# Moving the rank products behind the inverse transform, and reordering GpSimd's record and norm work around the wait for them

## The chip, the cores and the metric

The kernel runs on one core of one Trainium2 chip. The metric is the time of one execution on the device in microseconds (us), the median of several runs. Engines are named as in the profile: PE (TensorE matmuls), PEld (its weight loads), DVE (VectorE), ACT (ScalarE), POOL (GpSimd), SP (SyncE, which only issues transfers here).

## The reference, cut to what matters

```python
# x (64, 256, 257, 2), K (512, 512), W (7, 160, 160)
coeff = complex(x[..., 0], x[..., 1]) * sqrt_eig
h = irfft(einsum('nlm,mlk->nkm', coeff, pct), n=512, norm='forward')   # (64, 256, 512)

xn = layernorm(h)                      # first norm
key = xn @ K
logits = tanh(key @ xn^T + bias)       # 256 x 256 for each of the 64 blocks
logits = (logits - 10000 * outside_band) * temperature
h = h + softmax(logits) @ xn

x2 = layernorm(h)                      # second norm
mask = (x2[..., 0] >= 0.5) & (x2[..., 1] >= 0.5)
# of the tokens in the mask: four argmax over 16 columns of (x2 > 0.5), and column 29,
# through a 7-layer network of width 160; its two rounded results, as one-hot vectors
# times 2, are added to columns 128 to 159
h = h + x2 + add_where_mask(mask, ...)
```

Only tokens in the mask need the network. So the kernel gathers a record of 40 numbers for each of them into a dense list in HBM, and runs the network over that list.

## The kernel before, in words

There are three stages, one after the other. `stage1_spectrum` computes the Legendre sums and writes the spectrum `spec` to HBM; it streams about 200 MB. `stage2_blocks` takes the 64 blocks (256 tokens by 512 numbers each, kept as two tiles of 128 rows) through the inverse transform, the first norm, the attention, the second norm and the output, and writes the records. `stage3_ffn` runs the network over the records and scatters its results. The change touches `stage2_blocks` alone.

Stage 2 is a software pipeline. Each engine has its own program, a function `slot(i, k, has)`, called for i = -2 to 66 (slots 7 to 58 in a hardware loop of four slots a turn; k = i mod 4 picks buffers). `has(n)` is true where block n exists. The order of the work within a slot is the order in which `slot` writes it, and every engine executes its own list strictly in that order; semaphores tie the engines together. In slot i the engines work on different blocks at once:

- PE (L504): the keys of block i (48 products), the rank products of block i-3 (`rank`, L475), the transposed probabilities of i-1 (`probs_T`), the inverse transform of i+2 (`inverse_dft`, 16 products), the transposed input of i+1 (`x_T`), attention times values of i-1 (`attend`), the logits of i (24 x 2 products).
- ACT (L529): tanh of the logits of i-1 (L534) into `th`; exponentials `pr` of i-1 (L541); `keyhi` of i (L547); the copy of the ranks of i-3 out of PSUM into `pos` (L553); `pThi` of i-1 (L557); `xnhi` of i+1 (L562); `od` of i+2 (L568); `xThi` of i+1 (L574); the output `o` of block i-2 (L587), which needs the second norm's scale `sc2` and shift `sh2` from POOL.
- DVE (L595): temperature and row maximum of `lg` (L601), then `h2` = attention plus `h` of i-2 (L612), `xn` of i+1 (L623), `keylo` (L630), `pTlo` (L637), statistics of `h2` (L644), the sums and differences `eo` of the transform (L652), mean and variance `mv2` of block i-2 (L660), `h` of i+2 (L667, L669, L672), `xTlo` (L680), its statistics (L689), `x2` (L697), `mv1` (L706), `wb` (L712), `xnlo` (L719), `v4` (L723).
- POOL (L738): `lg` = `th` + `band` of i-1 (L743); variance plus epsilon and its power -1/2 for the first norm (L748, L751); `nmx`, the negated maxima (L755); for block i-3 the mask and its running counts (L761 to L769: `above`, `mask3`, `acc3`); then the records of block i-3 (L775 to L806, see below); then for block i-2 the second norm's root and what ACT's output needs: `ve` (L811), `rstd2` (L814), `sc2` (L818), `off` (L819), `sh2` (L821).
- SP (L403): loads the next spectrum block and stores `o`.

The ranks: `rank` multiplies the mask of block i-3 by a triangle of ones and the running count by a matrix of ones, both of 3 columns, into the first three columns of the logits' PSUM tile `ps_l`. It waits for the mask counts of POOL (`pool_mask`) and for ACT having read the previous logits (`act_tanh`). ACT copies the result to `pos`. POOL turns it into the row number of each token's record:

```python
pool.wait_ge(dve_v4, n + 1)     # L780
pool.wait_ge(act_pos, n + 1)    # L781: the wait for the ranks
nom  = FAR - FAR * mask3        # L783 (tokens outside the mask go far out of bounds)
fidx = pos + nom                # L786
idx  = uint32(fidx)             # L789
rec[:, r4, :, 0] = rows         # L790, then L791, L793, L796: the record's other fields
rows += NLAT * 16               # L801
for t in range(TILES):          # two indirect transfers, L803
    indirect_dma(recs[idx[:, t]] <- rec[:, t])
```

Of the kernel before, what the change touches and what calls it, by code (L numbers as in the profile page):

```python
# [12 lines left out]
ALU = mybir.AluOpType  # L13
# [4 lines left out]
TILES = NLAT // P  # L18
# [22 lines left out]
def wait(eng, sem, value):  # L41

    if isinstance(value, int) and value <= 0:
        return
    eng.wait_ge(sem, value)
# [204 lines left out]
def stage2_blocks(nc, const, spec, recs, out):  # L250


    with ExitStack() as ctx:
# [126 lines left out]
        def settled(eng):  # L380

            eng.nop(nofuse=True)
# [40 lines left out]
        def _(pe):  # L423
# [51 lines left out]
            def rank(n, k):  # L475

                pe.wait_ge(pool_mask, n * 4 + 4)
                pe.wait_ge(act_tanh, n + 3 if not isinstance(n, int) else min(n + 3, NB))
                nc.tensor.matmul(ps_l[:, 0, 0:3], trib[:, :], mask3[:, k % 2, :], start=True, stop=False)
                nc.tensor.matmul(ps_l[:, 0, 0:3], ones[:, :], acc3[:, k % 2, :],  # L480
                                 start=False, stop=True).then_inc(pe_rank, 1)
# [22 lines left out]
            def slot(i, k, has):  # L504
                if has(i):
                    keys(i, k)
                if has(i - 3):
                    rank(i - 3, (k + 1) % 4)
                if has(i - 1):
                    probs_T(i - 1)  # L510
                if has(i + 2):
                    inverse_dft(i + 2, (k + 2) % 4)
                if has(i + 1):
                    x_T(i + 1, (k + 1) % 4)
                if has(i - 1):
                    attend(i - 1, (k + 3) % 4)
                if has(i):
                    logits(i, k)
# [8 lines left out]
        @block.scalar  # L527
        def _(act):
            def slot(i, k, has):  # L529
                if has(i - 1):  # L530

                    act.wait_ge(pe_logit, i)
                    wait(act, pool_l, i - 1)
                    nc.scalar.activation(th[:, :, :], ps_l[:, :, :], ACT.Tanh,  # L534
                                         bias=bias[:, 0:1]).then_inc(act_tanh, 1)

                    act.wait_ge(pool_nmx, i)
                    wait(act, pe_pT, i - 1)
                    wait(act, dve_rsum, i - 3)
                    for t in range(TILES):  # L540
                        nc.scalar.activation(pr[:, t, :], lg[:, t, :], ACT.Exp, bias=nmx[:, t:t + 1],  # L541
                                             accum_out=ssum[:, (k + 1) % 2, t:t + 1]).then_inc(act_exp, 1)
                if has(i):
                    for b in range(2):
                        act.wait_ge(pe_key, i * 2 + b + 1)
                        wait(act, pe_logit, i)
                        nc.scalar.copy(keyhi[:, 2 * b:2 * b + 2, :].rearrange("p e w -> p (e w)"),  # L547
                                       ps_kx[b][:, :]).then_inc(act_keyhi, 1)
                if has(i - 3):
                    n = i - 3  # L550
                    act.wait_ge(pe_rank, n + 1)
                    wait(act, pool_idx, (n - 1) * 3)
                    nc.scalar.copy(pos[:, (k + 1) % 2, :], ps_l[:, 0, 0:3]).then_inc(act_pos, 1)  # L553
                if has(i - 1):
                    act.wait_ge(pe_pT, i)
                    wait(act, pe_av, (i - 1) * 2)
                    nc.scalar.copy(pThi[:, :, :], ps_pT[:, :, :]).then_inc(act_pThi, 1)  # L557
                if has(i + 1):
                    n = i + 1
                    act.wait_ge(dve_xn, n * 2 + 2)  # L560
                    wait(act, pe_av, (n - 3) * 2)
                    nc.scalar.copy(xnhi[:, (k + 1) % 4], xn[:, (k + 1) % 2]).then_inc(act_xnhi, 1)  # L562
                if has(i + 2):
                    n = i + 2
                    for t in range(TILES):
                        act.wait_ge(pe_dft, n * 2 + t + 1)
                        wait(act, dve_eo, (n - 1) * 4 + 2 * t + 2)
                        nc.scalar.copy(od[:, t, :], ps_dft[t][:, HALF:NLON]).then_inc(act_od, 1)  # L568
                if has(i + 1):
                    n = i + 1  # L570
                    for t in range(TILES):
                        act.wait_ge(pe_xT, n * 2 + t + 1)
                        wait(act, pe_logit, n - 1)
                        nc.scalar.copy(xThi[:, (k + 1) % 2, :, t * P:(t + 1) * P],  # L574
                                       ps_kx[t][:, :].rearrange("p (d w) -> p d w", d=CH)).then_inc(act_xThi, 1)
                if has(i - 2):

                    n = i - 2
                    act.wait_ge(pool_sc2, n * 3 + 3)
                    act.wait_ge(dve_h2, n * 2 + 2)  # L580
                    wait(act, pool_rec, (n - 1) * 4)
                    if isinstance(n, int):
                        wait(act, out_stored[k % 2], 16 * (n // 2))
                    else:
                        act.wait_ge(out_stored[k % 2], n * 8 - 8 * (k % 2))
                    for t in range(TILES):
                        nc.scalar.activation(o[:, k % 2, t], h2[:, k % 2, t], ACT.Identity,  # L587
                                             bias=sh2[:, k % 2, t:t + 1],
                                             scale=sc2[:, k % 2, t:t + 1]).then_inc(act_out, 1)

            slots(nc.scalar, slot)
# [145 lines left out]
        def _(pool):  # L737
            def slot(i, k, has):  # L738
# [34 lines left out]
                if has(i - 3):  # L773

                    n, r4, r2 = i - 3, (k + 1) % 4, (k + 1) % 2  # L775
                    if isinstance(n, int):
                        wait(pool, rec_sent[r4], 32 * (n // 4))
                    else:
                        pool.wait_ge(rec_sent[r4], n * 8 - 8 * r4)
                    pool.wait_ge(dve_v4, n + 1)  # L780
                    pool.wait_ge(act_pos, n + 1)  # L781
                    settled(pool)
                    nc.gpsimd.tensor_scalar(nom[:, :], mask3[:, r2, 0:2], -FAR, FAR, ALU.mult,  # L783
                                            ALU.add).then_inc(pool_idx, 1)
                    pool.wait_ge(pool_idx, n * 3 + 1)
                    nc.gpsimd.tensor_tensor(fidx[:, :], pos[:, r2, 0:2], nom[:, :], ALU.add).then_inc(pool_idx, 1)  # L786
                    pool.wait_ge(pool_idx, n * 3 + 2)
                    settled(pool)
                    nc.gpsimd.tensor_copy(idx[:, r4, :], fidx[:, :]).then_inc(pool_idx, 1)  # L789
                    nc.gpsimd.tensor_copy(rec[:, r4, :, 0], rows[:, :]).then_inc(pool_rec, 1)  # L790
                    nc.gpsimd.tensor_copy(rec[:, r4, :, 1:5],  # L791
                                          v4[:, r2, :].rearrange("p (t g) -> p t g", t=TILES)).then_inc(pool_rec, 1)
                    nc.gpsimd.tensor_copy(rec[:, r4, :, 5], x2[:, r2, :, 29]).then_inc(pool_rec, 1)  # L793
                    pool.wait_ge(act_out, n * 2 + 2)
                    settled(pool)
                    nc.gpsimd.tensor_copy(rec[:, r4, :, 8:ROW],  # L796
                                          o[:, r2, :, OUT_LO:OUT_LO + OUT_W]).then_inc(pool_rec, 1)
                    pool.wait_ge(pool_rec, n * 4 + 4)
                    pool.wait_ge(pool_idx, n * 3 + 3)
                    settled(pool)  # L800
                    nc.gpsimd.tensor_scalar(rows[:, :], rows[:, :], float(NLAT * 16), None, ALU.add)  # L801
                    for t in range(TILES):
                        nc.gpsimd.indirect_dma_start(  # L803
                            out=recs[:, :], out_offset=bass.IndirectOffsetOnAxis(ap=idx[:, r4, t:t + 1], axis=0),
                            in_=rec[:, r4, t, :], in_offset=None, bounds_check=NB * NLAT - 1,
                            oob_is_err=False).then_inc(rec_sent[r4], 16)  # L806
                if has(i - 2):
                    n, r2 = i - 2, k % 2
                    pool.wait_ge(dve_mv2, n * 2 + 2)
# [10 lines left out]
                    pool.wait_ge(pool_sc2, n * 3 + 2)  # L820
                    nc.gpsimd.tensor_tensor(sh2[:, r2, :], dcT[:, :, bass.ds(n, 1)].rearrange("p t o -> p (t o)"), off[:, :],  # L821
                                            ALU.subtract).then_inc(pool_sc2, 1)

            pool.wait_ge(consts_set, 6)
            pool.wait_ge(dcT_set, 1)
# [441 lines left out]
```

## Time and profile before

| | us |
|---|---|
| median of 3 runs | 1552.46 (1550.82 to 1553.61) |
| the profiled execution, its own time | 1550.52 |
| its span, first to last instruction | 1548.7 |
| PE busy in the span | 1365.0 (88%) |
| DVE busy | 1083.5 (70%) |
| ACT busy | 669.4 (43%) |
| POOL busy | 617.1 (40%) |

The profile is of one execution. Times count from the start of its span; durations of single instructions are given in us or, where marked, ns. An engine that sits idle before an instruction is shown with the instruction that released it. PEclk is the TensorE clock that was granted, as a share of full speed. Stage 1 lasts until about 346 us, stage 2 until about 1339, stage 3 from there.

### The profile page before, as it was taken

The page shows a single profiled execution, that of the slowest core. Times are in us where ns is not written, and L with a number is a line of the kernel's source. Part 1 is how long each engine was busy: PE and PEld are TensorE (multiplying, and loading weights), DVE is VectorE, ACT ScalarE, POOL GpSimd, SP SyncE. Part 2 cuts the span into 40 slices and gives each one's busy share as a digit, 9 for nine tenths or more (in the row PEclk, how much of TensorE's full clock was granted, in tenths as well). Part 3 has the DMA queues.
Part 4 walks back from the last instruction along what each step waited for, and adds up shares of the span by engine and source line. Part 5 has one row for each costly group of instructions (what it writes and reads, how often), then busy time and mean ns, then how long its engine had stood idle before and what let it go on. Part 6 is the DMA issues. An engine that isn't in the chain of part 4 may idle for free. (4 is left out here: it accounts for less than half of the span.)

```text
span 1548.7 us, 31360 instructions
## 1 busy us (share of the span) xinstructions
PE 1365.0 (88%) x9261; PEld 1191.6 (77%) x9261; DVE 1083.5 (70%) x2565; ACT 669.4 (43%) x1373; POOL 617.1 (40%) x1598
## 2 busy tenths in 40 slices
PE   4778777857999999999999999999999997399993
PEld 3666666747999999999999999999999986255551
DVE  1322222216899999999999999999999996377772
ACT  1222222122454554554544544545455443277772
POOL 2000000001365566555655665556556655302332
PEclk9789999897999999999999999999999999599997
DMA  9999999972211222212111221122112101100000
GB/s 374 428 427 430 428 427 429 427 268 90 70 70 71 69 79 73 70 69 81 71 68 69 76 74 69 68 81 69 68 69 79 59 30 42 37 1 12 10 4 5
DMA packets 58747, 210.57 MB, mean 136 GB/s; under 512 B 9413, under 2 KB 12177, under 8 KB 46289
## 3 DMA queue, kind: packets, MB, share of 16 engines
q1 hardware_dynamic: 47360, 172.29, 28.5%
q10 hardware_dynamic: 5200, 33.62, 5.4%
q0 software_dynamic: 6144, 4.14, 1.0%
q8 instruction: 20, 0.33, 0.1%
q14 instruction: 23, 0.18, 0.0%
HBM read 138.73 MB, written 73.07 MB: 137 GB/s over the span
## 5 line engine op out<-in xcount | busy, mean ns | idle before, releaser
L188 PE MATMUL s1b<-pg,cg 128*128 128x256 f32 x1024 | 248.7, 405 | 88.5 <-DVE cg L139 78.3
L188 PEld LDWEIGHTS s1b<-pg,cg 128*128 128x128 f32 x1024 | 206.3, 204 | 130.5 <-ACT stage L216 36.8
L428 PE MATMUL ps_kx<-xThi,Khi 128*128 128x256 f32 x1024 | 283.7, 277 | 4.0 <-DVE xTlo L680 4.0
L429 PE MATMUL ps_kx<-xTlo,Khi 128*128 128x256 f32 x1024 | 283.4, 277 | 0.0
L430 PE MATMUL ps_kx<-xThi,Klo 128*128 128x256 f32 x1024 | 283.4, 277 | 0.0
L139 DVE TENSOR_TENSOR cg<-xg,se 128x2048 f32<-128x2048 f32 x32 | 73.3, 2292 | 233.4 <-DMA pg<-in_pct_dram 226.0
L587 ACT ACTIVATE o<-h,sh,sc 128x512 f32<-128x512 f32 x128 | 97.5, 809 | 286.6 <-POOL sh L821 286.6
L428 PEld LDWEIGHTS ps_kx<-xThi,Khi 128*128 128x128 f32 x1024 | 193.2, 189 | 4.6 <-DVE xTlo L680 4.6
L429 PEld LDWEIGHTS ps_kx<-xTlo,Khi 128*128 128x128 f32 x1024 | 192.9, 188 | 0.0
L430 PEld LDWEIGHTS ps_kx<-xThi,Klo 128*128 128x128 f32 x1024 | 192.9, 188 | 0.0
L216 ACT COPY stage<-s1b 128x512 f32<-128x512 f32 x128 | 65.7, 598 | 234.3 <-PE s1b L188 234.3
L748 POOL TENSOR_SCALAR ve<-mv 128x2 f32<-128x2 f32 x64 | 15.9, 248 | 361.5 <-DVE mv L706 356.4
L743 POOL TENSOR_TENSOR lg<-th,band 128x512 f32<-128x512 f32 x64 | 90.2, 1409 | 169.9 <-ACT th L534 169.9
L803 POOL DMA_INDIRECT recs<-rec,idx x128 | 132.8, 1038 | 54.6 <-issue 54.3
L541 ACT ACTIVATE pr<-lg,nmx 128x256 f32<-128x256 f32 x128 | 64.1, 502 | 193.3 <-POOL nmx L755 193.3
L430 PE MATMUL ps_l<-xThi,keylo 128*128 128x256 f32 x512 | 144.9, 283 | 0.0
L429 PE MATMUL ps_l<-xTlo,keyhi 128*128 128x256 f32 x512 | 144.9, 283 | 0.0
L428 PE MATMUL ps_l<-xThi,keyhi 128*128 128x256 f32 x512 | 144.6, 282 | 0.0
L460 PE MATMUL ps_dft<-dft,xt 128*128 128x128 f32 (+2 forms) x1024 | 127.3, 278 | 2.9 <-DMA xt<-spec 2.9
L460 PEld LDWEIGHTS ps_dft<-dft,xt 128*128 128x128 f32 x1024 | 121.9, 195 | 3.0 <-issue 3.0
L1015 ACT ACTIVATE act_f<-ps_main,fb 128x512 f32<-128x512 f32 x150 | 96.2, 694 | 48.7 <-PE ps_main L1088 42.4
L428 PE MATMUL ps_av<-xnhi,pThi 128*128 128x512 f32 x256 | 106.8, 417 | 3.2 <-issue 1.7
(139 smaller groups left out, 3151.8 us busy)
## 6 DMA issues: line engine op xcount, KB each, us to landing
pg<-in_pct_dram SPq DMA_DIRECT2D x32, 2048.0 KB, 27.6
xg<-in_xs_dram SPq DMA_DIRECT2D x32, 1024.0 KB, 22.8
spec<-stage ACTq DMA_DIRECT2D x64, 512.0 KB, 8.5
xt<-spec SPq DMA_DIRECT2D x64, 512.0 KB, 3.6
out_dram<-o SPq DMA_DIRECT2D x64, 512.0 KB, 2.8
recs<-rec POOLq DMA_DIRECT2D x16, 160.0 KB, 16.5
recs<-rec,idx POOLq DMA_INDIRECT x128, 2.3
Kf<-in_K_dram SPq DMA_DIRECT2D x1, 1024.0 KB, 23.3
```

The costliest lines, as they stand in the source:

```text
L139: nc.vector.tensor_tensor(cg[:, b % 2], xg[:, b], se_view(g), ALU.mult).then_inc(scaled, 1)
L188: last = nc.tensor.matmul(bank[(b % 2) * 4 + m // 2][:, m % 2, :], cg[:, b % 2, m * 2 + h, :], pg[:, b, m * 2 + h, :], start=(h == 0), sto ...
L216: nc.scalar.copy(stage[:, b % 2, 2 * j:2 * j + 2, :], bank[(b % 2) * 4 + j][:, :, :]).then_inc(copied, 1)
L428: nc.tensor.matmul(out_ap, whi, mhi, start=(j == 0), stop=False)
L429: nc.tensor.matmul(out_ap, whi, mlo, start=False, stop=False)
L430: last = nc.tensor.matmul(out_ap, wlo, mhi, start=False, stop=(j == n - 1))
L460: last = nc.tensor.matmul(ps_dft[t][:, cols[0]:cols[1]], xt[:, k, src, t * P:(t + 1) * P], dft[:, cols[0]:cols[1]], start=True, stop=True)
L541: nc.scalar.activation(pr[:, t, :], lg[:, t, :], ACT.Exp, bias=nmx[:, t:t + 1], accum_out=ssum[:, (k + 1) % 2, t:t + 1]).then_inc(act_exp, 1)
L587: nc.scalar.activation(o[:, k % 2, t], h2[:, k % 2, t], ACT.Identity, bias=sh2[:, k % 2, t:t + 1], scale=sc2[:, k % 2, t:t + 1]).then_inc( ...
L743: nc.gpsimd.tensor_tensor(lg[:, :, :], th[:, :, :], band[:, :, :], ALU.add).then_inc(pool_l, 1)
L803: nc.gpsimd.indirect_dma_start(out=recs[:, :], out_offset=bass.IndirectOffsetOnAxis(ap=idx[:, r4, t:t + 1], axis=0), in_=rec[:, r4, t, :], ...
L1015: nc.scalar.activation(act_f[:, L % 2, g], ps_main[g][:, :], ACT.Relu, bias=fb[:, col:col + 1]).then_inc(act_relu, 1)
```

## The change

PE, ACT and POOL get another order within a slot of stage 2; DVE and SP keep theirs, and no operation is added or dropped.

- PE: `rank(i - 3)` moves from ahead of `probs_T` to behind `inverse_dft`, ahead of `x_T`.
- ACT: the copy `pos` (L553) moves from behind `keyhi` to behind `od`, ahead of `xThi`.
- POOL: behind the mask counts now come `nom` and the four copies into the record, without a wait for the ranks; then the second norm's group for block i-2 (`ve`, `rstd2`, `sc2`, `off`, `sh2`); and only then the wait for the ranks, `fidx`, `idx`, the step of `rows` and the two indirect transfers. The next instruction of POOL is `lg` of the next slot.

```diff
--- before.py
+++ after.py
@@ -504,12 +504,12 @@
             def slot(i, k, has):
                 if has(i):
                     keys(i, k)
-                if has(i - 3):
-                    rank(i - 3, (k + 1) % 4)
                 if has(i - 1):
                     probs_T(i - 1)
                 if has(i + 2):
                     inverse_dft(i + 2, (k + 2) % 4)
+                if has(i - 3):
+                    rank(i - 3, (k + 1) % 4)
                 if has(i + 1):
                     x_T(i + 1, (k + 1) % 4)
                 if has(i - 1):
@@ -546,11 +546,6 @@
                         wait(act, pe_logit, i)
                         nc.scalar.copy(keyhi[:, 2 * b:2 * b + 2, :].rearrange("p e w -> p (e w)"),
                                        ps_kx[b][:, :]).then_inc(act_keyhi, 1)
-                if has(i - 3):
-                    n = i - 3
-                    act.wait_ge(pe_rank, n + 1)
-                    wait(act, pool_idx, (n - 1) * 3)
-                    nc.scalar.copy(pos[:, (k + 1) % 2, :], ps_l[:, 0, 0:3]).then_inc(act_pos, 1)
                 if has(i - 1):
                     act.wait_ge(pe_pT, i)
                     wait(act, pe_av, (i - 1) * 2)
@@ -566,6 +561,11 @@
                         act.wait_ge(pe_dft, n * 2 + t + 1)
                         wait(act, dve_eo, (n - 1) * 4 + 2 * t + 2)
                         nc.scalar.copy(od[:, t, :], ps_dft[t][:, HALF:NLON]).then_inc(act_od, 1)
+                if has(i - 3):
+                    n = i - 3
+                    act.wait_ge(pe_rank, n + 1)
+                    wait(act, pool_idx, (n - 1) * 3)
+                    nc.scalar.copy(pos[:, (k + 1) % 2, :], ps_l[:, 0, 0:3]).then_inc(act_pos, 1)
                 if has(i + 1):
                     n = i + 1
                     for t in range(TILES):
@@ -777,17 +777,12 @@
                         wait(pool, rec_sent[r4], 32 * (n // 4))
                     else:
                         pool.wait_ge(rec_sent[r4], n * 8 - 8 * r4)
-                    pool.wait_ge(dve_v4, n + 1)
-                    pool.wait_ge(act_pos, n + 1)
                     settled(pool)
                     nc.gpsimd.tensor_scalar(nom[:, :], mask3[:, r2, 0:2], -FAR, FAR, ALU.mult,
                                             ALU.add).then_inc(pool_idx, 1)
-                    pool.wait_ge(pool_idx, n * 3 + 1)
-                    nc.gpsimd.tensor_tensor(fidx[:, :], pos[:, r2, 0:2], nom[:, :], ALU.add).then_inc(pool_idx, 1)
-                    pool.wait_ge(pool_idx, n * 3 + 2)
+                    nc.gpsimd.tensor_copy(rec[:, r4, :, 0], rows[:, :]).then_inc(pool_rec, 1)
+                    pool.wait_ge(dve_v4, n + 1)
                     settled(pool)
-                    nc.gpsimd.tensor_copy(idx[:, r4, :], fidx[:, :]).then_inc(pool_idx, 1)
-                    nc.gpsimd.tensor_copy(rec[:, r4, :, 0], rows[:, :]).then_inc(pool_rec, 1)
                     nc.gpsimd.tensor_copy(rec[:, r4, :, 1:5],
                                           v4[:, r2, :].rearrange("p (t g) -> p t g", t=TILES)).then_inc(pool_rec, 1)
                     nc.gpsimd.tensor_copy(rec[:, r4, :, 5], x2[:, r2, :, 29]).then_inc(pool_rec, 1)
@@ -795,15 +790,6 @@
                     settled(pool)
                     nc.gpsimd.tensor_copy(rec[:, r4, :, 8:ROW],
                                           o[:, r2, :, OUT_LO:OUT_LO + OUT_W]).then_inc(pool_rec, 1)
-                    pool.wait_ge(pool_rec, n * 4 + 4)
-                    pool.wait_ge(pool_idx, n * 3 + 3)
-                    settled(pool)
-                    nc.gpsimd.tensor_scalar(rows[:, :], rows[:, :], float(NLAT * 16), None, ALU.add)
-                    for t in range(TILES):
-                        nc.gpsimd.indirect_dma_start(
-                            out=recs[:, :], out_offset=bass.IndirectOffsetOnAxis(ap=idx[:, r4, t:t + 1], axis=0),
-                            in_=rec[:, r4, t, :], in_offset=None, bounds_check=NB * NLAT - 1,
-                            oob_is_err=False).then_inc(rec_sent[r4], 16)
                 if has(i - 2):
                     n, r2 = i - 2, k % 2
                     pool.wait_ge(dve_mv2, n * 2 + 2)
@@ -820,6 +806,23 @@
                     pool.wait_ge(pool_sc2, n * 3 + 2)
                     nc.gpsimd.tensor_tensor(sh2[:, r2, :], dcT[:, :, bass.ds(n, 1)].rearrange("p t o -> p (t o)"), off[:, :],
                                             ALU.subtract).then_inc(pool_sc2, 1)
+                if has(i - 3):
+                    n, r4, r2 = i - 3, (k + 1) % 4, (k + 1) % 2
+                    pool.wait_ge(act_pos, n + 1)
+                    pool.wait_ge(pool_idx, n * 3 + 1)
+                    nc.gpsimd.tensor_tensor(fidx[:, :], pos[:, r2, 0:2], nom[:, :], ALU.add).then_inc(pool_idx, 1)
+                    pool.wait_ge(pool_idx, n * 3 + 2)
+                    settled(pool)
+                    nc.gpsimd.tensor_copy(idx[:, r4, :], fidx[:, :]).then_inc(pool_idx, 1)
+                    pool.wait_ge(pool_rec, n * 4 + 4)
+                    pool.wait_ge(pool_idx, n * 3 + 3)
+                    settled(pool)
+                    nc.gpsimd.tensor_scalar(rows[:, :], rows[:, :], float(NLAT * 16), None, ALU.add)
+                    for t in range(TILES):
+                        nc.gpsimd.indirect_dma_start(
+                            out=recs[:, :], out_offset=bass.IndirectOffsetOnAxis(ap=idx[:, r4, t:t + 1], axis=0),
+                            in_=rec[:, r4, t, :], in_offset=None, bounds_check=NB * NLAT - 1,
+                            oob_is_err=False).then_inc(rec_sent[r4], 16)
 
             pool.wait_ge(consts_set, 6)
             pool.wait_ge(dcT_set, 1)
```

## Rows read from the trace of the kernel before

**Rows 1.** Busy time by stretch: start:end, length, each engine's busy us (instructions), clock, DMA share.

```profile
0.00:346.00 346.00, 249.56 (x1028) 207.06 (x1028) 79.54 (x40) 71.06 (x134) 8.95 (x20) 0.92 0.98 406
...
409.00:1280.00 871.00, 854.48 (x6731) 812.92 (x6731) 803.64 (x2066) 432.77 (x945) 518.70 (x1416) 1.00 0.20 70
```

**Rows 2.** Waits, 409 to 1280 us: who waited for whom, total us, times, longest.

```profile
ACT o L587 <- POOL sh L821: 259.7, 59, 5.7
...
POOL nom L783 <- ACT pos L553: 73.9, 59, 1.3
DVE lg L601 <- POOL lg L743: 61.2, 59, 2.1
...
PEld ps_l L479 <- POOL acc L769: 27.5, 57, 1.6
```

**Rows 3.** Timeline of POOL in one slot: start us, duration us, instruction [idle before <-releaser].

```profile
896.28 1.36 POOL L743 TENSOR_TENSOR lg<-th,band 128x512 f32<-128x512 f32 x1 [2.44 <-ACT th L534]
...
901.47 0.19 POOL L783 TENSOR_SCALAR nom<-mask 128x2 f32<-128x2 bf16 x1 [1.24 <-ACT pos L553]
901.74 0.19 POOL L786 TENSOR_TENSOR fidx<-pos,nom 128x2 f32<-128x2 f32 x1
902.07 0.19 POOL L789 CAST idx<-fidx 128x2 uint32<-128x2 f32 x1
...
903.05 0.23 POOL L801 TENSOR_SCALAR rows<-rows 128x2 f32<-128x2 f32 x1 [0.24 <-POOL rec L796]
903.79 1.10 POOL L803 DMA_INDIRECT recs<-rec,idx  x1 [0.52 <-issue]
905.19 0.97 POOL L803 DMA_INDIRECT recs<-rec,idx  x1 [0.30 <-issue]
906.24 0.60 POOL L811 TENSOR_SCALAR ve<-mv 128x2 f32<-128x2 f32 x1
...
908.39 0.19 POOL L821 TENSOR_TENSOR sh<-dcT,off 128x2 f32<-128x2 f32 x1 [0.17 <-POOL off L819]
911.02 1.36 POOL L743 TENSOR_TENSOR lg<-th,band 128x512 f32<-128x512 f32 x1 [2.44 <-ACT th L534]
```

**Rows 4.** Timeline of ACT, the same slot.

```profile
903.28 1.08 ACT L574 CAST xThi<-ps_kx 128x512 fp32r<-128x512 f32 x2
908.84 1.52 ACT L587 ACTIVATE o<-h,sh,sc 128x512 f32<-128x512 f32 x2 [4.49 <-POOL sh L821]
910.27 0.67 ACT L534 ACTIVATE th<-ps_l,bias 128x512 f32<-128x512 f32 x1
```

**Rows 5.** Timeline of DVE, the same slot.

```profile
905.32 0.24 DVE L660 BATCH_NORM_AGGREGATE mv<-bn 128x2 f32<-128x6 f32 x2
...
910.02 1.21 DVE L719 TENSOR_TENSOR xnlo<-xn,xnhi 128x1024 fp32r<-128x1024 f32 x1
```

**Rows 6.** Timeline of POOL: slot 2 (no records yet), the starts of slots 3 and 62.

```profile
404.44 0.50 POOL L811 TENSOR_SCALAR ve<-mv 128x2 f32<-128x2 f32 x1 [6.68 <-DVE mv L660]
...
406.63 0.19 POOL L821 TENSOR_TENSOR sh<-dcT,off 128x2 f32<-128x2 f32 x1
409.22 1.89 POOL L743 TENSOR_TENSOR lg<-th,band 128x512 f32<-128x512 f32 x1 [2.39 <-ACT th L534]
...
1280.34 1.69 POOL L743 TENSOR_TENSOR lg<-th,band 128x512 f32<-128x512 f32 x1 [2.21 <-ACT th L534]
```

**Rows 7.** Timeline of DVE, slot 2.

```profile
404.04 0.24 DVE L660 BATCH_NORM_AGGREGATE mv<-bn 128x2 f32<-128x6 f32 x2
404.20 0.65 DVE L667 TENSOR_TENSOR h<-eo 128x508 f32<-128x508 f32 x1
```

**Rows 8.** Timeline of POOL, a second transfer in slot 3, and `lg` of slot 63.

```profile
418.76 1.00 POOL L803 DMA_INDIRECT recs<-rec,idx  x1 [0.30 <-issue]
...
1294.80 1.29 POOL L743 TENSOR_TENSOR lg<-th,band 128x512 f32<-128x512 f32 x1 [2.21 <-ACT th L534]
```

**Rows 9.** Timeline of DVE, slot 3.

```profile
418.84 0.65 DVE L667 TENSOR_TENSOR h<-eo 128x508 f32<-128x508 f32 x1
```

## The prediction

> **What bounds the kernel now.** I read the busy times by stretch first. From 409 to 1280 us, more than half of the run, PE is busy 854.48 of 871 us [rows 1]. That looks like a kernel bound by its matmuls, with 871 - 854.5 = 16.5 us to be had at most. The starts of `lg` in slots 3 and 62 stand at 409.22 and 1280.34 [rows 6], 59 slots apart, so a slot lasts 14.77 us on the mean, and PE's own work in it is 854.48 / 59 = 14.48 us.
>
> Then the waits, to see which loop sets the 14.77. PE's weight loader waits 27.5 us in 57 slots for the mask counts of POOL [rows 2], so PE, full as it is, does not set the pace. ACT waits 4.4 us a slot (259.7 / 59) for `sh2`, POOL waits 1.25 us a slot for ACT's copy `pos`, DVE waits 1.04 us a slot for `lg` [rows 2]. The timeline shows how these close to one loop, of which POOL is the larger part. I take the slot that starts at 896.28 and measure from the start of its `lg`; it lasts 14.74 us, near the mean. Masks and exponentials come after `lg`, then ACT's `keyhi` and `pos`. POOL goes on with `nom` at 5.19, its two transfers start at 7.51 and 8.91, `ve` at 9.96, `sh` ends at 12.30 (908.58) [rows 3]. ACT starts `o` at 12.56 and `th` at 13.99 [rows 4], and the next `lg` starts at 14.74. All links follow on each other with gaps of a few tenths. So POOL's order matters in every slot, which is why this change can move the time at all.
>
> **What the change takes off that loop.** The wait of 1.24 us in front of `nom` [rows 3] goes, since `nom` no longer asks for the ranks. The record copies come ahead of it. And `ve` to `sh` no longer stand behind the two transfers. `sh` will then be late for another reason: `ve` needs `mv2` of DVE, and DVE's list is as it was. DVE begins its list when `lg` is there (`lg` ends at 897.64) and finishes `mv2` at 905.56 [rows 3, 5]. That is 9.28 us from the start of `lg`, while `ve` starts at 9.96 now. So the root can come forward by some 0.7 us at most, not by the 4.8 us of work that is cleared from in front of it. In between POOL stands idle.
>
> **What it adds to the loop.** The next instruction on POOL's list behind the second transfer is now `lg` of the next slot. Before, the block of `idx` and the transfers lay between the masks and `mv2`, in time that POOL would for the most part have had to wait for DVE anyway. Now that time is idle, and the block stands between `sh` and `lg`. So a new loop arises: `lg`, DVE's list to `mv2`, the root, the block, `lg`. Its length, step by step, from the start of `lg`:
>
> 1. To the end of `mv2`: 9.28 [rows 3, 5]. `lg` itself took 1.36 there, beside the end of DVE's `xnlo` (910.02 to 911.23 in the next slot); with DVE idle it took 1.29 [rows 3, 5, 8]. The later `lg` of the new order finds DVE idle, so 9.28 - 0.07 = 9.21.
> 2. The root. Slot 2 shows exactly the new situation: no records yet, POOL idle until `mv2` comes [rows 6]. From the end of `mv2` (404.04 + 0.24 = 404.28) to the end of `sh` (406.63 + 0.19 = 406.82) it took 2.54 us [rows 6, 7]. In the slot of 896.28 the same five instructions took 908.58 - 906.24 = 2.34 [rows 3]. I take 2.54, since it has the same DVE work beside it. Sum 11.75.
> 3. The block. `fidx` 0.08 behind `sh` (the gap between neighbours on POOL: the transfer ends at 906.16, `ve` starts at 906.24), 0.33 from `fidx` to `idx`, then 0.19 for `idx` and the 0.24 that `rows` waits, 0.74 from `rows` to the first transfer, 1.40 to the second, and 1.05 from that to the instruction behind it [rows 3]. Sum 4.03, which makes 15.78.
>
> The other way to the next `lg` goes through ACT: `sh` ends at 11.75, `o` starts 0.26 later and `th` 1.43 after that, `lg` 0.75 after `th` [rows 3, 4]. That gives 14.19, earlier than 15.78, so tanh will be ready and `lg` waits for POOL's own list. PE needs 14.48. The new loop is the longest: 15.78 against 14.77 us, 1.01 us a slot, in 59 slots: **59.6 us**.
>
> **The other parts.** On PE the two rank products move with their 0.1 us of issue, which costs PE the same in either place. Their wait for the masks disappears, because the masks are ready before the exponentials' work is done; what PE then waits for is the exponentials, later in each slot by the longer loop, 15.78 - 14.48 = 1.3 us a slot. Queued behind the rank now is `x_T`, later by that 0.1 us; with 1.3 us of idle time on PE this costs nothing. ACT's `pos` now comes just ahead of `xThi` (at 903.28, or 7.0 from `lg` [rows 4]); POOL asks for it at 11.8, so 4.8 us cover it. The record copies and `nom` need `rec_sent` of four slots ago, `v4` and `o` of the slot before, all past; their 0.2 us each lie in POOL's idle time. The transfers start 5.8 us later in the slot; they are waited for four slots later only. SP's queue is passed by nothing.
>
> At the ends: in slots 62 and 63 DVE's list is shorter and the new loop no longer than the old (nothing, down to -0.5 us each). In the last two slots the masks stand behind the block of the slot before, and the last record is late by between nothing and one block, 4.0 us; I take +1.5 us for it all. The sum is 1550.52 (the profiled execution's own time) + 59.6 + 1.5 = 1611.6 us. The median of the runs shown lies 1.9 us above that execution, so I forecast **1614 us**.
>
> **A rule weighed.** `ve` in slot 2 took 0.50 us, beside DVE's `h` (L667, 404.20 to 404.85) [rows 6, 7], more than twice the 0.22 that `rows`, an instruction of the same kind and size, takes [rows 3]. It looks like a wait for DVE. The Trainium skill (SBUF — State Buffer, Who interferes with whom) says that a DVE instruction with two SBUF inputs blocks a GpSimd instruction that reads SBUF, until its end. This speaks against the change, which puts `ve` right beside L667 and L669. By it the root takes 2.54, as slot 2 shows, and the time is the 1614 above; with the 2.34 of the later place in its stead it would be 0.2 x 59 = 12 us less, 1602.
>
> **Unknown costs, from both sides.** (a) The transfers move beside DVE's `x2` and `xnlo`. The nearest row is a second transfer at 418.76 beside L667: 1.00 instead of 0.97 us [rows 3, 8, 9], so I take nothing. The upper end is what `lg` lost in the same place, 1.89 against 1.29 [rows 6, 8]: +0.6 us a slot. No reason lets a transfer gain. (b) The copies move beside DVE's `xn` and may hold DVE: nothing, up to two of their 0.2 us, +0.4. Together +1.0 us a slot, 59 us. (c) On the low side the root could take 2.34 + 0.08 - 0.4 (if `ve` takes 0.2, not 0.60) = 2.0 instead of 2.54, and the block 0.1 less: -0.6 us a slot, -35 us. Together with the 1614 that makes 1579 at the low end and 1673 at the high one.
>
> **The rivals.**
> A. *Faster, PE becomes the bound.* This holds if the tail of the block runs beside `lg`, or is shorter than its rows: spans on POOL are rough, and a part of the 1.10 and 0.97 us may be work that POOL's list does not wait for. The loop must shrink by 15.78 - 14.48 = 1.3 us for it, a third of the block. Then a slot takes 14.48 and the time is the median's 1552 - 59 x 0.29 = 1535 us. Against it: `ve` starts 0.08 us behind the second transfer's end [rows 3], as if it had waited for it. 4%.
> B. *No change that can be measured.* The waits trade places one for one, or the move matters less than the edit says: 1.0 us a slot would have to vanish. About 1552 us. 2%.
> C. *Slower, with the port as a second cost.* The stretches of (a) and (b) come in full: 16.8 us a slot, about 1673 us. The section of the Trainium skill named above speaks for it as far as DVE's instructions with two SBUF inputs go; the 1.00 us of the one transfer seen beside such an instruction [rows 8, 9] speaks against it. 8%.
> D. *Slower, and TensorE loses its clock*, since PE now idles 1.3 us a slot. The granted clock was 1.00 in 409 to 1280 and 0.92 in stage 1, where PE was busy 249.56 of 346 us [rows 1]. At 0.92 PE's work takes 14.48 / 0.92 = 15.7 us, still inside 15.78, so a loss as large as stage 1's changes nothing. Only a longer stay at 1.2 GHz would show. At 0.85 the slot would be 17.0, about 1687 us. 2%.
> E. The forecast: 84%.
>
> **How the numbers follow.** The unknowns of E reach from 1579 to 1673, but their upper ends together are C. A range of 1580 to 1655 leaves out A and B (6%) below, C and D (10%) above and, as I judge, 4% of E: 8 times in 10 it holds. A measurement of this kernel tells a difference from 0.2% (3 us) on. Faster 0.04, same 0.02, slower 0.94.
>
> **What would show each step right or wrong.** In the profile after: the start-to-start time of `lg` is 15.8 us in slots 3 to 61; POOL's wait in front of `nom` for `pos` is gone, and there is one of about 4 us (from the copies' end near 5.2 to 9.3) in front of `ve`, released by DVE's `mv` (some 240 us in all); `lg` starts less than 0.1 us behind the second transfer and no longer waits for `th`; DVE's wait for `lg` rises from 1.0 to 2 us a slot; PE waits for `pr` instead of `acc`, about 1.3 us a slot, and its share of busy time in stage 2 falls from 98 to 92%. ACT's wait for `sh` falls by the half microsecond that `sh` comes earlier. The forecast is wrong if `lg` still waits for `th`, if the transfers overlap it, or if `mv2` comes well before 9.2 us.

## The result: 1617.4 us, a ratio of 1.042

The changed kernel takes 1617.4 us (median of 4 runs, 1616.7 to 1618.6) against 1552.8 for the kernel before: a ratio of 1.0419, 95% interval 1.0401 to 1.0437, 64.6 us slower. Taken again later beside other runs, it was 1616.1 us, ratio 1.0411 (1.0394 to 1.0428); this is e11 below. The forecast was 1614 us in a range of 1580 to 1655.

**The profile after.** Stretch 409 to 1280 us and the waits from 409 to 1340, in the columns of [rows 1] and [rows 2]:

```profile
409.00:1280.00 871.00, 801.26 (x6314) 762.05 (x6313) 753.79 (x1939) 403.84 (x883) 507.86 (x1324) 1.00 0.20 68
```

```profile
ACT pr L541 <- POOL nmx L755: 259.8, 59, 6.3
POOL ve L797 <- DVE mv L660: 245.3, 59, 4.4
ACT o L587 <- POOL sh L807: 238.7, 59, 4.2
DVE lg L601 <- POOL lg L743: 121.2, 59, 3.7
PEld ps_pT L449 <- ACT pr L541: 87.9, 58, 3.1
...
POOL lg L743 <- ACT th L534: 2.4, 1, 2.4
```

PE is busy 92% of the stretch in place of 98%. POOL's wait for `pos` is gone; in its place stand 4.2 us a slot in front of `ve`, for DVE's `mv2`. `lg` no longer waits for tanh, except once (2.4 us). DVE waits 2.05 us a slot for `lg`, twice as long as before.

POOL in one slot, and the `lg` of slots 3 and 62, as in [rows 3, 6]:

```profile
412.83 1.90 POOL L743 TENSOR_TENSOR lg<-th,band 128x512 f32<-128x512 f32 x1 [2.39 <-ACT th L534]
...
949.59 1.30 POOL L743 TENSOR_TENSOR lg<-th,band 128x512 f32<-128x512 f32 x1
...
954.48 0.23 POOL L791 COPY rec<-o 128x64 f32<-128x64 f32 x1
958.87 0.49 POOL L797 TENSOR_SCALAR ve<-mv 128x2 f32<-128x2 f32 x1 [4.16 <-DVE mv L660]
959.45 1.02 POOL L800 TENSOR_TENSOR rstd<-ve,mhalf 128x2 f32<-128x2 f32 x1
...
961.20 0.19 POOL L807 TENSOR_TENSOR sh<-dcT,off 128x2 f32<-128x2 f32 x1 [0.17 <-POOL off L805]
...
962.76 1.10 POOL L822 DMA_INDIRECT recs<-rec,idx  x1 [0.53 <-issue]
964.17 1.09 POOL L822 DMA_INDIRECT recs<-rec,idx  x1 [0.30 <-issue]
965.28 1.31 POOL L743 TENSOR_TENSOR lg<-th,band 128x512 f32<-128x512 f32 x1
...
1345.38 1.31 POOL L743 TENSOR_TENSOR lg<-th,band 128x512 f32<-128x512 f32 x1
```

And DVE and PE there:

```profile
958.47 0.24 DVE L660 BATCH_NORM_AGGREGATE mv<-bn 128x2 f32<-128x6 f32 x2
...
963.18 1.22 DVE L719 TENSOR_TENSOR xnlo<-xn,xnhi 128x1024 fp32r<-128x1024 f32 x1
```

```profile
953.51 0.66 PE L449 MATMUL ps_pT<-ident,pr 128*128 128x128 f32 x4 [1.28 <-ACT pr L541]
```

A slot now lasts (1345.38 - 412.83) / 59 = 15.81 us against 14.77, which makes 61.4 us over the 59 slots. Of the 67.3 us by which the two spans differ (1616.0 and 1548.7), 3.6 lie ahead of slot 3, in stage 1 and the filling of the pipeline (412.83 against 409.22), and 2.3 behind the start of slot 62 (270.6 against 268.4). The 3.6 are not the change's: in e11, the same kernel, slot 3 starts at 409.39.

### The profile page after: what moved, and what is told of

Read it like the earlier page. It is cut to its first block and busy times, and to the rows that moved or that the text cites. A ratio compares the mean times of both kernels' runs of the same rounds, so it can differ in the third digit from the quotient of the medians.

```text
span 1616.0 us, 31359 instructions
## 1 busy us (share of the span) xinstructions
PE 1363.9 (84%) x9261; PEld 1189.9 (74%) x9261; DVE 1083.5 (67%) x2565; ACT 667.3 (41%) x1373; POOL 643.4 (40%) x1598
## 5 line engine op out<-in xcount | busy, mean ns | idle before, releaser
L188 PE MATMUL s1b<-pg,cg 128*128 128x256 f32 x1024 | 245.3, 401 | 95.3 <-DVE cg L139 89.4
L748 POOL TENSOR_SCALAR ve<-mv 128x2 f32<-128x2 f32 x64 | 15.8, 247 | 364.8 <-DVE mv L706 359.5
L822 POOL DMA_INDIRECT recs<-rec,idx x128 | 139.0, 1086 | 55.1 <-issue 55.1
L601 DVE TENSOR_SCALAR_CACHE_REDUCE lg<-lg,temp 128x256 f32<-128x256 f32 x128 | 56.3, 477 | 135.1 <-POOL lg L743 135.1
L797 POOL TENSOR_SCALAR ve<-mv 128x2 f32<-128x2 f32 x64 | 30.7, 479 | 260.9 <-DVE mv L660 260.9
```

What stands on the lines that cost most here:

```text
L188: last = nc.tensor.matmul(bank[(b % 2) * 4 + m // 2][:, m % 2, :], cg[:, b % 2, m * 2 + h, :], pg[:, b, m * 2 + h, :], start=(h == 0), sto ...
L601: nc.vector.tensor_scalar(lg[:, t, :], lg[:, t, :], temp[:, 0:1], None, ALU.mult, ALU.max, accum_out=mx[:, t:t + 1]).then_inc(dve_max, 1)
L822: nc.gpsimd.indirect_dma_start(out=recs[:, :], out_offset=bass.IndirectOffsetOnAxis(ap=idx[:, r4, t:t + 1], axis=0), in_=rec[:, r4, t, :], ...
```

## The experiments

Ratios are against the kernel before, run on the same chip beside each. On the chip of e5 to e8 it took 1556.0 us, beside the other experiments 1553.6, beside the changed kernel 1552.8. So their ratios and the lengths of their slots are to be compared, not their times. The slot is measured as above, from the `lg` of slot 3 to that of slot 62, over 59.

| run | what it is | us | ratio (95%) | slot us |
|---|---|---|---|---|
| before | | 1552.8 | 1 | 14.77 |
| changed | | 1617.4 | 1.042 (1.040 to 1.044) | 15.81 |
| e1 | PE's and ACT's part alone | 1691.1 | 1.089 (1.086 to 1.091) | 17.03 |
| e2 | POOL's part alone | 1615.1 | 1.040 (1.038 to 1.042) | 15.81 |
| e3 | before, records filled first | 1547.9 | 0.996 (0.995 to 0.997) | 14.75 |
| e4 | changed, `mv2` early | 1610.5 | 1.037 (1.035 to 1.039) | 15.69 |
| e5 | e3, DVE reordered, `mv2` and `xnlo` early | 1538.1 | 0.988 (0.987 to 0.990) | 14.46 |
| e6 | e4, `xnlo` away from `lg` | 1599.1 | 1.028 (1.026 to 1.030) | 15.44 |
| e7 | changed, 1.4 us more in POOL's idle time | 1625.4 | 1.044 (1.042 to 1.047) | 15.81 |
| e8 | changed, 0.8 us more inside the block | 1698.3 | 1.091 (1.089 to 1.093) | 17.08 |
| e9 | before, DVE reordered | 1628.1 | 1.049 (1.047 to 1.050) | 16.02 |
| e10 | e3, DVE reordered as in e9 | 1527.9 | 0.984 (0.982 to 0.985) | 14.40 |
| e11 | changed, once more | 1616.1 | 1.041 (1.039 to 1.043) | 15.81 |

**e2 and e1: which part costs.** e2 takes the new `slot` of POOL with PE and ACT of before; e1 is the reverse.

> POOL in the changed order, PE and ACT as before. My theory: the whole loss sits in POOL's order (lg, DVE's list to mv2, root, block, lg), and PE and ACT have more than 1 us of slack in it, so lg starts every 15.8 us and the time is that of the change, 1617 us within 3. Rival (the move of the rank on PE and ACT carries part of the loss, or saves some): the time differs from 1617 by 0.1 us a slot or more, 6 us.

The slot is the changed kernel's, 15.81 us. The whole loss is in POOL's order; moving the rank and `pos` neither costs nor gains there.

> PE and ACT in the changed order, POOL in the order of before. My theory (the slot is the longest of a few loops through POOL): POOL's nom still waits for pos, and pos now comes behind od, about 6.9 us after the start of lg in place of 4.9, so the loop of before grows by 2.0 us a slot: about 16.75 us a slot, 1553 + 118 = 1671 us. Rival (PE is the bound and the wait for the mask counts on PE was the cost): 0.28 us a slot less, 1536 us. Second rival (the wait for pos moves under other work): 1553 us.

The run took 1691 us in place of 1671. Three slots of four were near the 16.75 (most of them 16.35 to 16.5 us), the fourth about 19. Of such a fourth slot, that of 954.73 us, PE and POOL:

```profile
958.79 1.11 PE L449 MATMUL ps_pT<-ident,pr 128*128 128x128 f32 x4 [2.14 <-ACT pr L541]
959.70 3.13 PE L460 MATMUL ps_dft<-dft,xt 128*128 128x129 f32 x16
```

```profile
963.62 0.19 POOL L783 TENSOR_SCALAR nom<-mask 128x2 f32<-128x2 bf16 x1 [4.94 <-ACT pos L568]
```

The busy time of 4 us that start within 0.7 us of the end of PE's pause, in an earlier slot (that of 527.86 us), in the slot before this one and in this one (the last three columns are the granted clock, the DMA share and GB/s):

```profile
532.40:536.40 4.00, 4.00 (x26) 3.99 (x25) 3.80 (x9) 2.60 (x6) 0.00 (x0) 0.61 0.00 0
942.20:946.20 4.00, 4.00 (x34) 3.86 (x35) 4.00 (x9) 3.99 (x9) 0.56 (x4) 1.00 0.11 10
958.80:962.80 4.00, 4.00 (x23) 3.99 (x24) 4.00 (x8) 2.79 (x5) 0.00 (x0) 0.58 0.00 0
```

PE had stood idle for 2.14 us (1.89 in the slot before, where the clock stayed at 1.00), and the granted clock fell to 0.58, most of the time the lower level of 1.2 GHz. The inverse transform took 3.13 us in place of 1.95, and since the ranks stood behind it, `pos` and POOL were late with it: `nom` starts 8.89 us from `lg`, in the slot before 7.14. POOL so comes beside DVE's `h`, where `idx` and the first copy took 0.65 us each in place of 0.19, another 0.9. The length of the pause alone does not decide whether the clock falls: in the slot of 527.86 us it fell to 0.61 behind a pause of 1.87 us, and behind the 2.91 us of the next slot it stayed at 1.00. What decides is open. This was rival D of the prediction, in a kernel that makes PE idle longer than the changed one does.

**e7 and e8: the same work in the idle time and in the block.**

```diff
+ for t in range(2):                  # e7, behind the record copies; e8 one, behind idx
+     nc.gpsimd.tensor_tensor(spare[:, t, :], rows[:, :], mhalf[:, :], ALU.pow)
```

> The change, with two powers on a spare tile (0.8 us each) added on POOL behind the record copies, in its idle time ahead of ve. Theory: about 4 us of idle time cover them; 1617 us, within 3. Rival (POOL's total work counts): 1617 + 59 * 1.6 = 1711 us.

> The change, with one such power added inside the block, between idx and rows. Theory: it lies on the loop, so each slot grows by its 0.8 us less the 0.15 that rows waits for idx now: 0.65 us, 1617 + 38 = 1655 us, and more if PE's longer idle time (2 us a slot) costs it its clock as in e1_pe_act_only. Rival (the block is partly beside other work): less than 20 us more.

e7's slot did not move (15.81 us), so the idle time covers it. The run is 8 us over the changed kernel's, outside the 3 forecast, but its slots hold nothing of them: its stage 3 took 6 us longer, as did those of e5, e6 and e8 on that chip, and by the ratios (1.044 and 1.042, whose intervals overlap) it can't be told from the changed kernel. e8 grew by 1.3 us a slot, twice the forecast. The first two fences are POOL and DVE in a late slot, the next two in slot 3:

```profile
950.18 0.80 POOL L818 TENSOR_TENSOR spare<-rows,mhalf 128x2 f32<-128x2 f32 x1
951.05 0.23 POOL L822 TENSOR_SCALAR rows<-rows 128x2 f32<-128x2 f32 x1
951.55 2.16 POOL L824 DMA_INDIRECT recs<-rec,idx  x1 [0.27 <-issue]
```

```profile
951.52 1.22 DVE L720 TENSOR_TENSOR xnlo<-xn,xnhi 128x1024 fp32r<-128x1024 f32 x1
```

```profile
423.39 1.13 POOL L824 DMA_INDIRECT recs<-rec,idx  x1 [0.28 <-issue]
```

```profile
423.57 1.21 DVE L720 TENSOR_TENSOR xnlo<-xn,xnhi 128x1024 fp32r<-128x1024 f32 x1
```

Where the transfer starts 0.18 us ahead of `xnlo` it takes 1.13 us, and that slot, of 16.48 us, is only 0.19 longer than slot 3 of the changed kernel (16.29; for slots 4 and 5 it is 15.83 against 15.65 and 15.68): the power is mostly hidden by waits of POOL's own (0.27 in place of 0.53 us ahead of the transfer, and `rows` no longer waits). Where the transfer starts 0.03 us behind `xnlo` it takes 2.16. In slot 6 it starts 0.02 us ahead (471.08 against 471.10) and takes 1.09. So most of e8's growth is this stretch, not the power.

The expectation named TensorE's clock as another way to grow, and in some slots of e8 it did fall. It isn't the cause. Slots 22 and 33 of e8 last 17.07 and 17.08 us, each with a pause of PE, of 2.60 and 2.67 us, and only the second lost the clock behind it:

```profile
736.20:740.20 4.00, 4.00 (x34) 3.77 (x33) 4.00 (x9) 3.60 (x8) 0.73 (x4) 1.00 0.16 44
925.30:929.30 4.00, 4.00 (x25) 3.94 (x24) 4.00 (x9) 2.52 (x6) 0.68 (x4) 0.57 0.00 0
```

**e4 and e6: the other end of the loop.** If the loop runs through `mv2`, an earlier `mv2` must shorten it.

```diff
  # e4, DVE's slot:                      # e6, DVE's slot, behind xTlo:
+ mv2 of i-2  (was behind eo)            + xnlo, x2, wb, statistics of h, v4, mv1
  eo of i+2
```

> The change, with DVE's mean and variance of the second norm moved ahead of eo. My theory: mv2 is there 1.2 us earlier, near 7.9 us; the root, now beside eo that reads one input from PSUM, takes 2.0 to 2.7 us, the block 3.9; the loop is 13.8 to 14.5 us and PE's 14.48 takes over: 1536 to 1540 us. Rival (what costs is the block itself or the held port, wherever mv2 lies, or lg waits for tanh): stays above 1600 us.

> e4_mv2_early (1610 us) with xnlo ahead of x2 and the statistics of h behind it, so that xnlo no longer meets lg. Theory: in e4 the loop through mv2 did shrink by about 1.3 us, but xnlo took 2.95 us in place of 1.22, because it stood behind lg at the shared port, and gave it back; without the meeting the slot is 14.5 to 14.8 us and the time 1537 to 1555 us. Rival (the block between root and lg costs its length wherever mv2 lies): stays near 1610 us.

e4 missed by 1.2 us a slot. DVE and POOL of e4 around the end of a slot:

```profile
956.98 2.95 DVE L719 TENSOR_TENSOR xnlo<-xn,xnhi 128x1024 fp32r<-128x1024 f32 x1
```

```profile
957.54 1.30 POOL L743 TENSOR_TENSOR lg<-th,band 128x512 f32<-128x512 f32 x1
958.93 1.09 POOL L748 TENSOR_SCALAR ve<-mv 128x2 f32<-128x2 f32 x1
```

`xnlo` takes 2.95 us in place of 1.22; it ends at 959.93, 1.09 us behind the end of `lg`, and only then does POOL's `ve` (0.22 us elsewhere) end. DVE is now busy 98% of the stretch and sets the slot itself. So the gain was given back at the port, for the most part: in slots 5 and 6 of e4 `xnlo` still took 1.22 us, and they last 14.95 and 14.93 us; from slot 8 on it takes 2.95, and a slot lasts 15.6 to 15.9. (Even those two are 0.45 above the forecast.) e6 takes `xnlo` away from `lg` and gains a part, 15.44 us. POOL of e6:

```profile
942.76 0.22 POOL L797 TENSOR_SCALAR ve<-mv 128x2 f32<-128x2 f32 x1 [2.97 <-DVE mv L651]
...
944.16 0.60 POOL L805 TENSOR_TENSOR off<-mv,rstd 128x2 f32<-128x2 f32 x1
944.93 0.42 POOL L807 TENSOR_TENSOR sh<-dcT,off 128x2 f32<-128x2 f32 x1 [0.17 <-POOL off L805]
...
946.72 1.96 POOL L822 DMA_INDIRECT recs<-rec,idx  x1 [0.53 <-issue]
948.98 0.98 POOL L822 DMA_INDIRECT recs<-rec,idx  x1 [0.30 <-issue]
```

`ve` starts 8.1 us from the start of `lg` (934.68), 1.2 earlier than in the changed kernel, as theory had it. But `xnlo` now runs from 946.50 to 947.71, and the first transfer, which starts in it, takes 1.96 us: 0.9 us is lost again. Step by step, the slot of 15.31 us is 7.92 to the end of `mv2` (9.12 in the changed kernel), 2.75 for the root (2.68) and 4.64 for the block (3.89). Still the forecast of e6, 14.5 to 14.8 us a slot, was missed, and its 1599 us lie nearer the rival's 1610. That the slot would be near 14.5 without the stretch is an estimate (15.31 - 0.86), which no run shows. The three parts show the loop as I said and where the gain went; the rival of an unavoidable cost of the block is not needed, but the time alone doesn't rule it out.

**e3, e9, e5, e10: what bounds the kernel before.** e3 keeps the block ahead of the root and moves only what needs no ranks ahead of the wait. The DVE order of e9 and e10 puts a one-input instruction beside `lg`.

```diff
  # e3 (POOL): nom, rec copies, then      # e9, e10 (DVE), behind xTlo:
- wait(act_pos); nom; fidx; idx; copies   - statistics of h, x2, mv1, wb, xnlo, v4
+ nom; copies; wait(act_pos); fidx; idx   + x2, xnlo, wb, statistics of h, v4, mv1
```

> Before, with only nom and the four record copies put ahead of the wait for pos; fidx, idx, rows and the transfers stay ahead of the root. My theory: the copies vanish in the wait; the transfers end 0.9 us earlier, ve then waits for mv2 (9.3 us), sh ends near 11.8, lg could start at 14.2, so PE's 14.48 us of work bounds the slot: 1553 - 0.28 * 59 = 1536 us. Rival (filling the records early is itself harmful, through DVE held by the copies): 1553 us or more.

The slot stayed at 14.75 us, where 14.48 was forecast. The waits of e3, 409 to 1280 us, show why I was wrong: `ve` has begun to wait for `mv2`, so the transfers do end early, and yet DVE waits for `lg` as before.

```profile
DVE lg L601 <- POOL lg L743: 60.7, 59, 1.6
...
PEld ps_l L479 <- POOL acc L769: 27.2, 58, 1.0
POOL ve L812 <- DVE mv L660: 23.5, 58, 0.6
```

DVE and POOL of e3 at the turn of a slot:

```profile
970.53 1.22 DVE L719 TENSOR_TENSOR xnlo<-xn,xnhi 128x1024 fp32r<-128x1024 f32 x1
```

```profile
971.19 1.71 POOL L743 TENSOR_TENSOR lg<-th,band 128x512 f32<-128x512 f32 x1 [2.44 <-ACT th L534]
```

`lg` starts 0.66 us behind the start of `xnlo`, 0.56 ahead of its end, and takes 1.71 us in place of 1.29. It ends 1.15 us behind `xnlo`, exactly as in before (911.23 to 912.38, [rows 3, 5]). POOL's own loop has become shorter: the `lg` before ended at 958.16, so from there to the start of this one it is 13.03 us, and with an `lg` of 1.29 us the slot would be 14.32. What holds it at 14.74 is a second loop, which in before ties with POOL's: DVE's list, then `lg`. Of the 5.7 us of e3 the 59 slots hold 0.6; its last slots, behind the start of slot 62, are 2.7 us shorter, and the rest isn't located.

> Before, PE, ACT and POOL untouched, with DVE's order changed behind xTlo: x2, xnlo, wb, the statistics of h, v4, mv1, so that lg meets an instruction with one SBUF input and not xnlo. Theory (two loops tie at 14.7 us in before: POOL with its wait for pos, and DVE's list with lg behind xnlo): relieving DVE's alone leaves POOL's, so at most 0.1 to 0.15 us a slot is gained, 0 to 9 us. Rival (DVE with lg alone set the pace, and POOL's loop merely followed): 14.5 us a slot, 16 us less than before.

> The same order on DVE together with POOL filling the records first (e3_fill_first). Theory: both loops are shorter than PE's work, a slot is 14.5 us, and the time is 16 to 20 us under before, as in e5_fill_first_port (ratio 0.988). Rival (x2 or xnlo holds sh at the port and the loop through o and tanh gets longer): between e3_fill_first (ratio 0.996) and before, or slower.

> The records filled first and the transfers ahead of the root, as in e3_fill_first (1547.9 us, lg still every 14.75 us), with DVE's order changed: mv2 and xnlo ahead of eo, x2 ahead of h, and the statistics of h (one SBUF input) last, beside lg. Theory from e3: what held the slot at 14.75 there, and as a tie before, is DVE's list plus lg, since lg can't run beside xnlo (two SBUF inputs): 13.55 us from the maxima to xnlo's end and 1.18 of lg behind it. Then lg now overlaps DVE, and PE's 14.48 us bound the slot: 1548 - 16 = 1532 us. Rival (PE's own wait for the masks, or tanh, sets 14.75): stays at 1548 us.

e9 went the other way: neither its theory (0 to 9 us faster) nor its rival held, and what happened is what the rival of e10 names, `sh` held at the port. POOL of e9, of e10, and DVE of each (e9 first):

```profile
950.59 1.49 POOL L821 TENSOR_TENSOR sh<-dcT,off 128x2 f32<-128x2 f32 x1 [0.17 <-POOL off L819]
```

```profile
942.45 0.26 POOL L822 TENSOR_TENSOR sh<-dcT,off 128x2 f32<-128x2 f32 x1 [0.17 <-POOL off L820]
```

```profile
950.02 0.59 DVE L691 TENSOR_SCALAR x<-h,mv,rstd 128x128 f32<-128x128 f32 x2
950.53 1.22 DVE L698 TENSOR_TENSOR xnlo<-xn,xnhi 128x1024 fp32r<-128x1024 f32 x1
```

```profile
942.32 0.59 DVE L691 TENSOR_SCALAR x<-h,mv,rstd 128x128 f32<-128x128 f32 x2
```

In e9 `sh` starts at 950.59, 0.06 us behind the start of `xnlo`, and ends 0.33 us behind its end: 1.49 us for an instruction of 0.19, on the very loop that bounds the kernel. The slot grows by the 1.3. In e10 the records are filled first, the slot of 930.54 has its `sh` at 11.91 from `lg` and the next, 945.15, at 11.70 (12.13 in e9), just behind the start of `x2`, and it takes 0.26. There both loops are short: 14.40 us a slot and 1527.9 us, ratio 0.984, the fastest of all and 25.6 us under before, more than the 16 to 20 forecast. e5 gets to 14.46, as forecast, with another order. e9 doesn't test the tie, since its reorder brought the meeting at the port; that there are two loops rests on e3, where POOL's was shortened without effect, and on e10 and e5, where both were.

The last expectation on record is that of the changed kernel's second measurement, told with the result.

> The changed kernel once more, beside these, so that its ratio is taken on the same chip: 1.042, between 1.040 and 1.044.

## Why the prediction was right, step by step

- **The end of `mv2`**, 9.21 forecast: 958.71 - 949.59 = 9.12 us. `lg` runs in 1.30 us, as taken from slot 63.
- **The root**, 2.54 from slot 2: 961.39 - 958.71 = 2.68. It starts with a `ve` of 0.49 us and a power of 1.02; slot 2 had shown 0.50 [rows 6] and 1.00.
- **The block**, 4.03: 965.28 - 961.39 = 3.89. `fidx` and `rows` wait a little less than in the old place; the second transfer takes 0.1 us more, 1.09 for 0.97.
- **The loop**, 15.78: 15.69 in this slot, 15.81 on the mean. Times 59: 59.6 forecast, 61.4 measured. That the mean is met within 0.03 us is in part luck: the slot worked out is 0.09 shorter than forecast, while every fourth slot lasts 16.0 us and slot 59 lasts 17.40. **The ends**, 1.5: 2.3.
- **Covered work.** `nom` and the copies end 5.1 us from `lg`, with 4.16 us of idle time behind them; e7 shows the cover. `pos` and the rank cost nothing, e2. The unknown (b) came out on POOL's side: a copy took 0.32 us beside DVE's `xn`, and DVE's `xn` took its 0.99.
- **PE's clock** stayed at 1.00, with pauses of 1.2 to 1.4 us in nearly every slot. In e1 and e8, with pauses of 1.87 us and more, it fell in some slots and not in others.
- **The rule of the port** held, for `ve` and the power. By it I should have looked further. The Trainium skill (SBUF — State Buffer, Who interferes with whom) excepts DVE's two-input instructions from those that hold up a software transfer's descriptors, as something inferred; in e6 and e8 a transfer that started inside `xnlo` took 1.96 and 2.16 us, so on this kernel an indirect transfer isn't excepted. Such a transfer also takes an index tile, and no run here separates the reading of it from the descriptors.
- **Unknown (a), the transfers beside `xnlo`.** In the changed kernel it cost the 0.1 us of the second transfer, which starts at 964.17, 0.23 us ahead of the end of `xnlo`. That it cost no more is luck. The first transfer starts 0.42 us ahead of `xnlo` (962.76 against 963.18). Had it started just behind, it would by e8 have taken 1.06 us more, 63 us over the slots: some 1680 us by this estimate, outside my range. The row from which I took nothing shows a transfer that started 0.08 us ahead of DVE's `h` (418.76 against 418.84 [rows 8, 9]); I read it as beside, and missed that the order of the starts decides. My upper bound of 0.6 us was too low as well: where the meeting came, it cost 0.9 (e6) and 1.06 us (e8).

What was wrong is a part that didn't enter the sum: **what bounds the kernel before**. I named one loop, through POOL, and wrote that PE's 14.48 us would be next, worth 16.5 us. e3 shows a second loop of the same length, DVE's list with `lg` behind `xnlo` at the port (13.55 us from the maxima to the end of `xnlo`, 1.18 to the next maxima). Nor was PE's floor 14.48: e10 runs at 14.40, with PE busy 847.50 of the 849.37 us of its 59 slots, 14.36 a slot. Before's busy time of 14.48 probably held small stretches of waiting, which no row separates. The forecast was spared this because the new loop is a whole microsecond longer than all of these.

## What to carry to other kernels

When a block is moved on an in-order queue, ask what the engine did in the time that the block filled: here it would have waited for `mv2` anyway, so the block was nearly free where it stood, and is on the loop, at its full 3.9 us, where it went. Taking a wait out of the front of a list gains only as much as the next input is early. And before a reorder that changes where GpSimd meets DVE, lay the two timelines over each other: 0.2 us decided here between 0.26 and 1.49 us for the same instruction (e10 and e9), and 0.05 us between 1.09 and 2.16 (e8).

## What I had not expected of the hardware

- An indirect transfer of GpSimd that starts while DVE runs `xnlo`, an instruction with two SBUF inputs, is held: in e6 and in e8 (1.96 and 2.16 us for 1.10) it ends 0.97 us behind `xnlo` each time. One that starts 0.02 us ahead isn't held (1.09).
- The waiting works both ways: DVE's `xnlo` took 2.95 us for 1.22 when it met `lg`.
- PE's granted clock fell behind a pause of 2.14 us (0.58 in the following 4 us) and behind one of 1.87 (0.61), and stayed at 1.00 behind others of 1.89, 2.60 and 2.91. The length of the pause alone doesn't tell.
